# Self-attention of a two-layer gated cross-attention block: the value products one step later in TensorE's order, the evictions of their outputs behind them

## The reference, cut to what matters

```python
B, S, D = x.shape                      # 2, 512, 512
h = _rms(x, ln_w)
q = (h @ wq).reshape(B, S, 32, 64)
k = (h @ wk).reshape(B, S, 8, 64)
v = (h @ wv).reshape(B, S, 8, 64)
q, k = _rope(q, k)
k = jnp.repeat(k, 4, axis=2)
v = jnp.repeat(v, 4, axis=2)
scores = jnp.einsum('bqhd,bkhd->bhqk', q, k) / 8.0
scores = jnp.where(causal[None, None], scores, -1e+30)
attn = jax.nn.softmax(scores, -1)
o = jnp.einsum('bhqk,bkhd->bqhd', attn, v).reshape(B, S, 2048)
x = x + o @ wo
```

## Time and profile before

| | |
|---|---|
| median of 3 runs | 2764.41 us (2759.43 to 2767.6) |
| the profiled execution | 2757.99 us, span 2756.2 us |
| granted TensorE clock, mean | 0.951 of full speed |
| PE busy | 2393.5 us (87%) |
| DVE / ACT / POOL busy | 1704.7 / 1487.0 / 1097.6 us |
| the self-attention in the trace | about 930 to 1560 us |

### The profile page before, as it was taken

One profiled execution on the slowest core, in us unless ns is written; L12 is line 12 of the kernel. 1 busy time (PEld: TensorE's weight loads), 2 busy tenths in 40 slices (PEclk: granted clock), 3 DMA queues, 4 the chain that ended last, 5 costly groups with the idle time before them and its releaser, 6 DMA issues.

```text
span 2756.2 us, 46217 instructions
## 1 busy us (share of the span) xinstructions
PE 2393.5 (87%) x14828; PEld 1987.5 (72%) x14828; DVE 1704.7 (62%) x3850; ACT 1487.0 (54%) x3094; POOL 1097.6 (40%) x1556
## 2 busy tenths in 40 slices
PE   5999999999995698989898664899998479889888
PEld 3777878878774688878887543899998367667754
DVE  2555555555555466666666474565565578778866
ACT  3644444444454566666666445444443477677765
POOL 0322222232320344444444246777765364444410
PEclk9999999999998799999999877999999789999999
DMA  3300000000023000000000237667675562242000
GB/s 131 111 30 8 19 11 13 13 13 18 8 84 130 12 21 19 19 19 19 3 16 19 79 118 226 186 190 188 188 203 131 137 187 58 50 92 65 9 5 31
DMA packets 147525, 198.38 MB, mean 72 GB/s; under 512 B 21924, under 2 KB 85796, under 8 KB 147044
## 3 DMA queue, kind: packets, MB, share of 16 engines
q1 hardware_dynamic: 131672, 160.70, 19.8%
q0 software_dynamic: 10992, 25.96, 4.4%
q10 hardware_dynamic: 4768, 10.62, 1.3%
HBM read 151.09 MB, written 46.15 MB: 72 GB/s over the span
## 4 chain that ended last, share of the span: by engine, by line
PE 69%; DVE 10%; ACT 7%; issue 6%; DMA 4%; POOL 3%; DVEq 0%; SPq 0%; ACTq 0%; POOLq 0%
PE pair L2271 8%; PE pair L655 6%; PE pair L1199 5%; PE pair L683 5%; PE pair L1249 5%; PE pair L2760 4%; PE pair L616 4%; PE pair L641 3%; PE pair L2289 3%; PE pair L1271 3%; PE pair L2743 3%; PE pair L672 2%; PE pair L1233 2%; PE pair L2775 2%; PE pair L622 2%
## 5 line engine op out<-in xcount | busy, mean ns | idle before, releaser
L531 ACT ACTIVATE x_p<-x_p,x_least 128x1024 f32<-128x1024 f32 x128 | 147.2, 1150 | 279.5 <-DVE x_least L482 279.5
L587 POOL TENSOR_TENSOR x_carry<-x_rtotal 128x1 f32<-128x1 f32 x128 | 24.7, 193 | 571.7 <-DVE x_rtotal L459 571.7
L466 DVE TENSOR_TENSOR x_pT<-pair,x_pT 128x512 fp32r<-128x512 f32 x256 | 164.2, 683 | 122.0 <-ACT x_pT L552 121.9
L2271 PE MATMUL pair<-m_h,e_w 128*128 128x320 f32 x1536 | 229.6, 310 | 1.1 <-DVE m_h L2186 1.1
L2271 PEld LDWEIGHTS pair<-m_h,e_w 128*128 128x128 f32 x1536 | 228.1, 189 | 2.7 <-issue 1.5
L655 PE MATMUL pair<-x_pT,x_v 128*128 128x256 f32 x1536 | 210.9, 295 | 14.4 <-DVE x_pT L466 14.4
L655 PEld LDWEIGHTS pair<-x_pT,x_v 128*128 128x128 f32 x1536 | 195.2, 195 | 31.6 <-issue 22.0
L1111 ACT ACTIVATE s_p<-s_p,s_least 128x128 f32<-128x128 f32 (+3 forms) x256 | 143.6, 561 | 123.1 <-DVE s_least L1021 123.1
L683 PE MATMUL pair<-x_kT,x_qT 128*128 128x512 f32 x768 | 207.0, 404 | 0.0
L2666 DVE TENSOR_REDUCE z_most<-pair 128x1 f32<-128x1008 f32 x128 | 153.9, 1202 | 83.9 <-PE pair L2785 52.1
L1249 PE MATMUL pair<-s_pT,s_v 128*128 128x256 f32 (+1 forms) x1152 | 158.8, 284 | 47.4 <-DVE s_pT L998 47.4
(11 more groups left out here) (351 smaller groups left out, 6100.8 us busy)
## 6 DMA issues: line engine op xcount, KB each, us to landing
e_raw<-in_L_ffn_w SPq DMA_DIRECT2D x48, 1024.0 KB
z_kS<-z_k SPq DMA_DIRECT2D x24, 512.0 KB, 9.4
hslot<-in_L_ffn_w ACTq DMA_DIRECT2D x16, 512.0 KB, 3.5
hT_x<-in_L_ffn_w SPq DMA_DIRECT2D x16, 512.0 KB, 5.5
z_v<-z_vst SPq DMA_DIRECT2D x16, 512.0 KB, 3.0
z_vS<-z_v SPq DMA_DIRECT2D x8, 960.0 KB, 5.1
z_qS<-z_q SPq DMA_DIRECT2D x24, 256.0 KB, 4.2
s_wraw<-in_L_ffn_wq SPq DMA_DIRECT2D x9, 512.0 KB, 4.5
```

Source lines behind the costliest of these rows:

```text
L466: dve.tensor_tensor(pT[1][:, keys, q * P:(q + 1) * P], TR[j][:, :].rearrange("p (k n) -> p k n", n=P), pT[0][:, keys, q * P:(q + 1) * P].b ...
L531: act.activation(p[n][:, :], p[n][:, :], ACT.Exp, scale=-1.0, bias=least[:, n:n + 1], accum_out=total[:, n:n + 1]).then_inc(s_ex, 1)
L2271: mm = pe.matmul(GU[m % 2][:, j * BANK:j * BANK + CAP], w[x0][:, c, m * P:(m + 1) * P], XS[s][x1][:, c, :], start=(n == 0 and c == 0), sto ...
```

## The change

The step of values(m) becomes LAG + 4 + 2m = 9 + 2m. values(0) to values(3) stand at steps 9, 11, 13, 15, and values(4) to values(7) at steps 1, 3, 5, 7 of the next turn. PAIR_DONE becomes 15, so outputs(0) stands at the end of ACT's step 15 and outputs(1) at step 7 of the next turn. low_outputs(1) moves to step 8 on DVE, and low_outputs(0), which would have stood at step 16, to step 0 of the next turn. No instruction is added or taken away, and no DMA moves.

```diff
-            PAIR_DONE = PAIR + LAG + 1
+            PAIR_DONE = PAIR + LAG + 2
             OUT = (9, 10, 11, 12)
-            assert PAIR_DONE + PAIR - NS < OUT[0] and B * PAIR <= NS
+            assert PAIR_DONE == NS - 1 and PAIR_DONE + PAIR - NS < OUT[0] and B * PAIR <= NS
...
                         if before and n == PAIR_DONE + PAIR - NS + 1:
                             low_outputs(PPB - 1, h - 1)
-                        if own and n == PAIR_DONE + 1:
-                            low_outputs(0, h)
+                        if before and n == PAIR_DONE + 1 - NS:
+                            low_outputs(0, h - 1)
...
-                        m = (n - LAG - 3) // 2
-                        if (n - LAG - 3) % 2 == 0:
+                        m = (n - LAG - 4) // 2
+                        if (n - LAG - 4) % 2 == 0:
                             if m >= 0 and own:
                                 values(m, h, b)
                             elif m < 0 and before:
```

## The result

The changed kernel took 2769.9 us in the median of 20 runs (2764.34 to 2775.68), the kernel before 2763.5 in 20 runs beside it (2758.89 to 2767.68): a ratio of 1.0025 with a 95% interval of 1.0017 to 1.0032. The forecast was no change that can be told. The kernel became slower, clear of the noise, though by few us, and the time lies inside the range.

What follows compares the result with a forecast made beforehand. It took TensorE, busy 558 of 630 us in the self-attention, and its waits, largest for low (47.4 us), as the bound. Terms 1.3 - 6.6 + 4.8 = -0.5 gave 2763 us, no change that can be told, range 2747 to 2777.

Steps and rivals of the forecast that it cites:

- The waits: Steps 4 to 9: t inherits values' wait for low; project_out(0) newly waits for low_outputs(1), 1.2 to 2.2 us.
- the walk: Trace intervals followed through a pair of turns at full clock: step 10 scores 0.57 (b = 1) and 0.24 us (b = 0) later.
- Rival 1: Loop turns: waits for low really go because low_outputs(1) isn't late; 2736 us, chance 0.15.
- rival 2: b = 1 turns: rotated(0) gets ahead of POOL's product, 1.15 us off the path seven times; 2755 us, chance 0.10.
- rival 4: Whole change: waits only change their names, in the ends as well; +1.3, 2766 us, chance 0.07.
- The steady pair: Two loop turns, b = 1 and b = 0, at full clock: +0.19 us a pair, +1.3 us over seven pairs.
- the stacks: Steps 12 to 1, stack(2), stack(4) and project_in(0): 0.31 us won per turn, bounds -0.3 and 1.08.
- The ends: Last turn and tail: 2.8 us won of the waits for low, 3.8 in the tail, together -6.6 us.
- The clock: Waits in 14 loop turns: falls at 6 places instead of 3, 1.59 us each; +4.8 us, bounds -4.8 and +17.5.
- rival 3: project_out(0)'s wait drops the clock every turn, +17.5, 2777 us; decides from 12 hits of 14; chance 0.18.

Runs made afterwards that it cites:

- fill_after: Changed kernel plus idle transposes in the step 8 and 9 waits: 12 in b = 0 turns, 12 and 6 in b = 1 turns; 2750.66 us, 0.9947 of before.
- ends_only: Kernel before with the new order only in the last turn and the tail; 2750.76 us, 0.9949 of before.
- fill_control: Kernel before plus 6 idle transposes ahead of values(7) at step 6 of the loop turns; 2762.10 us, 1.0000 of before.
- evict_early: Changed kernel with outputs(1) ahead of exp(7) on ACT and low_outputs(1) between low(1) and rotated(1) on DVE; 2737.82 us, 0.9902 of before.
- wo_early_after: Changed kernel with ACT's copies and POOL's products of the `wo` weights one step earlier in b = 1 turns; 2754.17 us, 0.9972 of before.
- wo_early_before: Kernel before with ACT's copies and POOL's products of the `wo` weights one step earlier in b = 1 turns; 2762.54 us, 1.0002 of before.
- wo_early_ends: Kernel before with the new order only in last turn and tail, and the `wo` weights one step earlier; 2754.69 us, 0.9973 of before.
- fill_b0: Changed kernel plus 12 idle transposes between t(3) and project_out(0) in b = 0 turns alone; 2761.13 us, 0.9998 of before.

## Why the prediction was wrong, point by point

**The waits: right.** Against the start of rotated(0), in the b = 1 turn with a full clock, t(3) starts where the walk has it (1064.13 against 1064.14, in the time of rows 3) and low_outputs(1) too (1065.01 against 1065.04). project_out(0) comes 0.16 later than walked, since from the end of low_outputs(1) to PE it is 0.23 and not 0.05, and the scores of step 10 0.79 later than before instead of 0.57. In the b = 0 turns the wait of project_out(0) is 1.95 (walked 2.2), behind a wait of t(3) of 0.51. Rival 1 (the waits go) falls, rival 2 (rotated(0) gets ahead) falls with the 1.96, and rival 4 falls with the ends.

**The steady pair: mis-sized, +0.52 instead of +0.19.** The b = 0 turn came out as worked (38.82 to 38.73, -0.09; the terms give 0.24 - 0.31 = -0.07). The b = 1 turn costs 0.60 instead of 0.26: the 0.79 above, less about 0.2 won at the stacks and behind them instead of 0.31. In the 13 turns that is +3.6 where the term had +1.3.

**The ends: right within a us.** The order is worth 5.8 at the end where I had 6.6, and 1.3 in the first turn, where I had booked nothing. The table has 1.75 there, but 0.5 of it come back behind the last project_in(0) (74.72 to the last project_outs in fill_after, 74.25 in ends_only), since in the new order values(4) stands behind project_in(0) and not ahead of it. The first turn takes 35.4 to 35.7 in all six kernels with the old order there and 33.4 to 33.6 in all six with the new one.

**The clock: the step that failed.** "At the same share 6 are hit, 3 more: +4.8 us." 13 of 14 were hit. In the 13 turns this costs 18.5 instead of 4.4, and the fourteenth place 1.6 (76.29 to the last project_outs where fill_after has 74.72): +15.6. At the very end the clock gave back 3.8: before had lost 5.35 there (91.16 - 80.08 - 5.73), the changed kernel loses 1.5 (7.25 - 5.73). Together +11.8 instead of +4.8. I had carried a share of 3 in 7, counted at single waits of 2.2, to places of another kind: two waits with 0.63 us of transposes between them. That was rival 3, with its mechanism and its point of decision (12 of 14), and it should have had more than 0.18. fill_after shows it by itself: the same order, with the waits filled, is some 20 us faster.

**The sum.** +3.6 for the order in the 13 turns, -1.3 in the first turn, -5.8 at the end, +11.8 for the clock: +8.3, which is what the self-attention grew by in the profiles. The medians moved by 6.4. That the number is no further off is in part luck: the first turn's 1.3 and the 3.8 of clock at the end stood in no term, and both went against the failed one. And 20 runs on each side do tell 0.25%, where I had drawn the line at 0.3%.

Where the change's own gain went: at a full clock it is 3.5 us faster than before, and 11.8 go into the clock. What it needed was its two evictions in time: values, t and the evictions form one chain, and the change moved outputs(1) behind exp(7) and low_outputs(1) behind rotated(1) just where project_out(0) waits. With those two moved forward the new order beats the old one by 27 us, 14 of which the ends alone give (ends_only), and by 40 with `wo` one step earlier; the old order gets nothing from that last edit.

## What to carry to other kernels

When a product is moved from behind a wait to ahead of it, look which instruction inherits the wait and what eviction the product fed: move that eviction to the earliest place where its input is ready, on both engines, in the same edit. Give the clock a term of its own for each place where TensorE is left with little to do, and take its size from a trace of that very pattern: here two waits close together lost about 1.5 us at 13 of 14 places, where a single wait of 2.20 had lost it at 3 of 7. A share counted at one kind of gap doesn't carry to another. An instruction moved away from one it contends with lands beside the next: read which one before booking the gain.

## What the runs showed of the hardware that I had not expected

- The falls aren't scattered in most of the kernels. In before, fill_control, ends_only, evict_early and wo_early_after the b = 1 turns in which the clock fell are the same three: the first, fourth and seventh. One wait of 2.2 us (before), one of 1.79 (evict_early) and 1.12 with 1.18 behind it (wo_early_after) all gave 3 of 7; 1.79 with 1.18 behind it gave 6 of 7, and 0.51 with 1.95 behind it 6 of 6. In wo_early_before they are the first, sixth and seventh, in wo_early_ends the first, second, fifth and sixth. And they keep an even distance: in the changed kernel they begin 40.96 us apart wherever no place is skipped, though its turns take 41.2 and 40.3 in alternation, and in before 235.52 us apart. So a share such as 3 of 7 may say as much of how a kernel's places fall in with that rhythm as of how long its waits are. What sets the rhythm stays open.
- 12 idle transposes (1.47 us of the 1.79) and 6 (0.82 of the 1.18) keep a granted clock of 1.00 over 500 us at almost no cost (turns of 39.73 to 39.77 against 39.70 in the one turn whose clock stayed up without them).
- A fall costs about 1.5 us here, but where only the b = 0 places were filled (fill_b0), four of seven b = 1 turns lost 2.3 to 2.8 us (41.98 to 42.51 against 39.72), and one in wo_early_before lost 3.0 (42.38 against 39.4).
- POOL is slowed in its turn: its product took 1.54 us in wo_early_before, where it began 0.22 behind a rotate, and 1.28 in before, where rotated(0) came 0.01 behind it.
